# Outer products of two token tiles: one block-diagonal product of 128 rows, or two products of 64 rows

## What is computed

```
scores, idx = top_k(sim, K)                       # 8 of 32 keys, in each of two halves
all_scores = scores[0][..., :, None] + scores[1][..., None, :]
all_idx = idx[0][..., :, None] * NK + idx[1][..., None, :]
sc, pk = top_k(all_scores, K)
indices = take_along_axis(all_idx, pk)            # 64 experts of a token (8 heads x 8)
hmid = einsum('bnd,bnhkd->bnhk', inputs, down[indices])
hmid = sigmoid(sc) * gelu(hmid)
out = einsum('bnhk,bnhkd->bnd', hmid, up[indices])
```

## Time and profile before

| | |
|---|---|
| median of 3 runs | 543.69 us (541.75 to 544.99) |
| profiled execution | 543.2 us, span 541.4 us |
| busy, share of the span | PE 82%, PEld 64%, DVE 75%, ACT 40%, POOL 27% |
| experts, from the first to the last spread | 338.7 to 532.0 us |
| one steady duo | 32.0 us |
| matmuls of the spread | 2 x 896 in the records, mean 192 ns each from start to end |

### The profile page before, as it was taken

One profiled execution on the slowest core, in us unless ns is written; L12 is line 12 of the kernel. 1 busy time (PEld: TensorE's weight loads), 2 busy tenths in 40 slices (PEclk: granted clock), 3 DMA queues, 4 the chain that ended last, 5 costly groups with the idle time before them and its releaser, 6 DMA issues. The chain is left out here.

```text
span 541.4 us, 14245 instructions
## 1 busy us (share of the span) xinstructions
PE 442.6 (82%) x5223; PEld 348.8 (64%) x5223; DVE 407.6 (75%) x1693; ACT 216.7 (40%) x401; POOL 147.4 (27%) x206
## 2 busy tenths in 40 slices
PE   1889999978999999999998534967849587684867
PEld 1667777765688687787777222756638376573767
DVE  2899999967455465455466699999899979999571
ACT  1454554566445345345464304232242423224230
POOL 1343334430000000000000153461726537163600
PEclk9999999999999999999998858585765858668596
DMA  9991000010356646646100000000000000000000
GB/s 222 219 217 48 0 0 0 10 70 1 95 136 146 193 116 163 177 114 179 49 2 1 0 1 0 4 10 3 12 1 3 10 2 10 1 11 2 3 11 11
DMA packets 8730, 30.51 MB, mean 56 GB/s; under 512 B 696, under 2 KB 4280, under 8 KB 8408
## 3 DMA queue, kind: packets, MB, share of 16 engines
q1 hardware_dynamic: 8680, 29.89, 21.9%
HBM read 28.97 MB, written 0.92 MB: 55 GB/s over the span
## 5 line engine op out<-in xcount | busy, mean ns | idle before, releaser
L1274 PE MATMUL PS<-b_hi,AR 128*128 128x16 f16 x896 | 54.8, 192 | 25.0 <-DVEq L936 25.0
L1274 PEld LDWEIGHTS PS<-b_hi,AR 128*128 128x128 f16 x896 | 54.0, 108 | 29.0 <-DVEq L936 29.0
L1244 PE MATMUL PS<-xlT,KB 128*128 (+1 forms) x112 | 35.1, 467 | 26.9 <-ACT AR L594 22.1
L1275 PE MATMUL PS<-b_lo,AR 128*128 128x16 f16 x896 | 54.7, 192 | 0.0
L1275 PEld LDWEIGHTS PS<-b_lo,AR 128*128 128x128 f16 x896 | 54.1, 107 | 0.0
L1244 PEld LDWEIGHTS PS<-xlT,KB 128*128 128x128 f32 x112 | 24.5, 230 | 38.3 <-ACT AR L594 24.9
L1070 PE MATMUL PS<-KA,AR 125*128 125x125 f32 x384 | 46.8, 272 | 0.8 <-ACT AR L417 0.8
L343 POOL TENSOR_TENSOR xn<-xn,cexp 128x1280 f16<-128x1280 f16 x14 | 41.8, 2985 | 17.8 <-DVE xn L907 17.8
L1154 PE MATMUL PS<-AR 125*64 125x128 f32 x768 | 46.6, 279 | 0.0
L1136 PE MATMUL PS<-AR 128*64 128x500 f32 x192 | 43.8, 591 | 1.3 <-ACT XA L499 0.9
L1070 PEld LDWEIGHTS PS<-KA,AR 125*128 125x128 f32 x384 | 41.6, 141 | 4.7 <-issue 3.5
(11 more groups left out here) (146 smaller groups left out, 980.6 us busy)
## 6 DMA issues: line engine op xcount, KB each, us to landing
AR<-ctx SPq DMA_DIRECT2D x16, 1344.0 KB
AR<-ctx SPq DMA_DIRECT2D x16, 156.0 KB
KB<-pack_b SPq DMA_DIRECT2D x1, 1280.0 KB, 13.6
XA<-pack_q SPq DMA_DIRECT2D x1, 1024.0 KB, 4.7
KA<-pack_a SPq DMA_DIRECT2D x1, 965.0 KB, 6.8
XA<-x SPq DMA_DIRECT2D x4, 224.0 KB
out<-res SPq DMA_DIRECT2D x7, 128.0 KB, 1.8
XA<-zeros SPq DMA_DIRECT2D x2, 64.0 KB
```

The lines of the kernel that those rows point to most:

```text
L1244: last = mm(bank(6 + r % 2, k * 256, k * 256 + 256), wb("down")[:, v * U:(v + 1) * U], xlT[:, bass.ds(i * 2 * TILE, 2 * TILE)], **one)
L1274: mm(o, pick_u[:, n, :], b_hi[:, :, n], start=True, stop=False)
L1275: last = mm(o, pick_u[:, n, :], b_lo[:, :, n], start=False, stop=True)
```

## The change

The two tiles' outer products are computed apart. `b_hi` and `b_lo` shrink to 8 columns per n and have no zero quarters, so POOL's two fills go and DVE fills each with one instruction over 128 partitions. For each n `spread` issues four matmuls: b_hi for rows 0 to 63, b_hi for rows 64 to 127, then both for b_lo. Each loads 64 rows of pick_u (128 columns) as weights and has 8 columns. The first tile's results go to banks 0 and 1, the second's to banks 2 and 3, 64 n in each bank. ACT's four copies and DVE's last scaling follow that layout: the copies keep their number and size; the scaling becomes four instructions of 512 elements for eight of 256, behind two signals for four.

```diff
-        b_hi = sb("b_hi", [128, 2 * V, TILE], F16)
-        b_lo = sb("b_lo", [128, 2 * V, TILE], F16)
+        b_hi = sb("b_hi", [128, V, TILE], F16)
+        b_lo = sb("b_lo", [128, V, TILE], F16)
...
-            ch.did(nc.gpsimd.memset(b_hi[:, :, :], 0.0))
-            ch.did(nc.gpsimd.memset(b_lo[:, :, :], 0.0))
...
             def mix_copies(i):
                 act.wait_ge(s["mix_psum"], i + 2)
                 for b in range(4):
-                    last = nc.scalar.activation(act_w[:, :, :, b * 32:(b + 1) * 32].rearrange("p t v n -> p (t v) n"),
-                                                bank(b).rearrange("p (n w) -> p w n", w=2 * V), ACT.Copy, scale=1.0 / W_UP)
+                    last = nc.scalar.activation(act_w[:, b // 2, :, (b % 2) * 64:(b % 2) * 64 + 64],
+                                                bank(b).rearrange("p (n v) -> p v n", v=V), ACT.Copy, scale=1.0 / W_UP)
...
-                for t in range(2):
-                    for dst, w in ((b_hi, w_hi), (b_lo, w_lo)):
-                        r = slice(t * HK, (t + 1) * HK)
-                        ch.did(nc.vector.tensor_tensor(dst[r, t * V:(t + 1) * V, :], pick_v[r, :, :],
-                                                       w[r, :].rearrange("p (o n) -> p o n", o=1).to_broadcast([HK, V, TILE]), ALU.mult))
+                for dst, w in ((b_hi, w_hi), (b_lo, w_lo)):
+                    ch.did(nc.vector.tensor_tensor(dst[:, :, :], pick_v[:, :, :],
+                                                   w[:, :].rearrange("p (o n) -> p o n", o=1).to_broadcast([128, V, TILE]), ALU.mult))
...
-            for b in range(4):
-                dve.wait_ge(s["bank_spread"], b + 1)
+            for half in range(2):
+                dve.wait_ge(s["bank_spread"], half + 1)
                 for t in range(2):
-                    n0 = (DUOS - 1) * 2 * TILE + t * TILE + b * 32
+                    n0 = (DUOS - 1) * 2 * TILE + t * TILE + half * 64
                     last = nc.vector.scalar_tensor_tensor(
-                        act_w[:, t, :, b * 32:(b + 1) * 32], bank(b).rearrange("p (n t v) -> p t v n", t=2, v=V)[:, t], 1.0 / W_UP,
-                        gelu[:, :, n0:n0 + 32], ALU.mult, ALU.mult)
+                        act_w[:, t, :, half * 64:half * 64 + 64], bank(2 * t + half).rearrange("p (n v) -> p v n", v=V), 1.0 / W_UP,
+                        gelu[:, :, n0:n0 + 64], ALU.mult, ALU.mult)
...
                 for n in range(TILE):
-                    o = bank(n // 32, (n % 32) * 16, (n % 32) * 16 + 16)
-                    mm(o, pick_u[:, n, :], b_hi[:, :, n], start=True, stop=False)
-                    last = mm(o, pick_u[:, n, :], b_lo[:, :, n], start=False, stop=True)
-                    if by_bank and n % 32 == 31:
+                    for dst, stop in ((b_hi, False), (b_lo, True)):
+                        for t in range(2):
+                            r = slice(t * HK, (t + 1) * HK)
+                            last = mm(bank(2 * t + n // 64, (n % 64) * V, (n % 64) * V + V), pick_u[r, n, :], dst[r, :, n],
+                                      start=not stop, stop=stop)
+                    if by_bank and n % 64 == 63:
                         last.then_inc(s["bank_spread"], 1)
```

More of the change, by code:

```diff
@@ L951, in _ @@
             with dve.Fori(0, (DUOS - 1) // 2) as i:
-                ch.enter(i, 2 * (2 * (16 + 16 + 4 + 8 + 8) + 3 + 2 + 4 + U // V - 1))
+                ch.enter(i, 2 * (2 * (16 + 16 + 4 + 8 + 8) + 3 + 2 + 2 + U // V - 1))
                 for j in range(2):
@@ L959, in _ @@
             dve.wait_ge(s["h_done"], (V // 2) * DUOS)
-            for b in range(4):
-                dve.wait_ge(s["bank_spread"], b + 1)
+            for half in range(2):
+                dve.wait_ge(s["bank_spread"], half + 1)
                 for t in range(2):
-                    n0 = (DUOS - 1) * 2 * TILE + t * TILE + b * 32
+                    n0 = (DUOS - 1) * 2 * TILE + t * TILE + half * 64
                     last = nc.vector.scalar_tensor_tensor(
-                        act_w[:, t, :, b * 32:(b + 1) * 32], bank(b).rearrange("p (n t v) -> p t v n", t=2, v=V)[:, t], 1.0 / W_UP,
-                        gelu[:, :, n0:n0 + 32], ALU.mult, ALU.mult)
-                    last.then_inc(s["mixed" if b == 3 else "dve"], 1)
-                    ch.n += b < 3
-                if b == 2:
+                        act_w[:, t, :, half * 64:half * 64 + 64], bank(2 * t + half).rearrange("p (n v) -> p v n", v=V), 1.0 / W_UP,
+                        gelu[:, :, n0:n0 + 64], ALU.mult, ALU.mult)
+                    last.then_inc(s["mixed" if half else "dve"], 1)
+                    ch.n += 1 - half
+                if half == 0:
                     ch.wait()
```

## The result

| | before | after |
|---|---|---|
| median of 4 runs | 543.61 us (541.75 to 544.99) | 548.98 us (548.63 to 549.29) |
| profiled span | 541.4 us | 547.4 us |
| busy, share of the span | PE 82%, DVE 75%, POOL 27% | PE 79%, DVE 72%, POOL 27% |

The ratio is 1.0101, with a 95% interval of 1.0070 to 1.0132: slower by 1.0%, 5.4 us where 21 were forecast. In the changed kernel the spread is L1272, the two products that fill b_hi and b_lo are L927, pick_u is L930, POOL's hit is L341 (L343 before) and its `mix` L353 (L355 before).

A forecast was written before the change was run, and what follows sets the result against it. It took DVE's chain, held by POOL's `mix`, to bound the pass. Terms -1.33 + 8.7 + 5.74 + 8.0 = +21.1 us on the 543.2 us profiled run gave 564.3, hence about 564.8 us by the median; range 536 to 576.

The forecast's parts named there:

- Nothing overlaps there. I therefore take 30.0 ns per pair: PE's spread: row halves do not run side by side, so 512 load-and-matmul pairs take 15.38 us against 7.69.
- Rival B: PE's spread at a pace between, 23 to 28 ns per pair: 11.8 to 14.3 us, total 540 to 557; chance 0.08.
- Rival A: PE's row halves overlap, the spread stays 7.7 us, only DVE's gain is left: 534.5 us; chance 0.20.
- The chain by `mix`: Steady pass from spread start s: POOL's `mix` follows the longer spread, ends at s + 22.33, holds DVE; pass 33.82 against 32.08.
- rival C: The spread doubles but the later `mix` does not hold DVE; picks start earlier, total 553 to 558 us; chance 0.09.
- The working: Step-by-step timing of spread, copies, `mix`, keys and picks, giving a steady pass of 33.82 us at a 15.38 us spread.
- first spread: Start of the first duo's spread: earlier by 1.33 us through DVE's two fewer instructions.
- five steady passes: The five like passes from one spread's start to the next: +1.74 us each, +8.7 in all.
- sixth pass: The shorter pass before the last spread: later `mix` delays picks by 7.07 us, less 1.33, so +5.74.
- tail: After the last spread's start: the spread lies bare, +7.69, and the final scaling adds at most 0.34; +8.0 us.
- The slope of 7 us per us of spread: Each microsecond of spread counts seven times: in five passes, the sixth and the end of the run.
- the break-even of 24.2 ns: PE's pace per pair at which the forecast's sign turns, a spread of 12.37 us.

The follow-up runs named there:

- the run with 8 columns: The kernel before with TensorE's loop over duos 1 to 6, one duo per pass, each spread matmul using only 8 of its 16 columns; 541.29 us.
- before in the same loop: The kernel before, with TensorE's loop over all duos 1 to 6, one duo per pass; 541.80 us, ratio to before 0.9979.
- the four products come back: The changed kernel with TensorE's loop over all duos 1 to 6, VectorE again making the factors in four 64-partition products; 542.60 us, ratio to before 1.0009.
- the block kernel: Changed kernel, TensorE looping one duo per pass; except in the last duo, the spread does all first-half-row products, then all of the other half; 555.41 us.
- the run with half of `mix`: The kernel with one duo per pass and the spread's row halves in blocks, with POOL's `mix` multiplying only half of its columns; 540.38 us.
- the kernel with two duos per pass: The changed kernel with TensorE's loop over all duos 1 to 6, written as three passes of two duos instead of one duo per pass; 549.93 us.
- the loop of one duo: The changed kernel with TensorE's loop written with one duo per pass instead of two, duos 1 to 4 in it; 543.09 us, ratio to before 1.0004.

## Why the prediction was wrong, step by step

**The step that failed: "Nothing overlaps there. I therefore take 30.0 ns per pair".** The spread's term was mis-sized in two ways, one against the other: forecast 15.38 us, measured 11.7 to 13.1. First, the array takes 13.3 ns per matmul, not 30.0, and the spread is 6.8 us where the instructions are there. The rows that I took for the nearest were pairs on alternating *column* halves in f32; row halves in f16 do overlap. Whether the type or the kind of tile makes that difference, no run shows. The Trainium skill (TensorEngine Tiling (Array Packing), Key Properties) says that different tiles load and multiply in parallel; for row tiles the traces agree, 13.3 ns in alternation against 26.5 in blocks. I gave that rule 0.20, on rows of another kind of tile.

Of the 30.0 ns itself 3.4 belong to the 8 columns that fell away, as the run with 8 columns shows; I had read that 16 columns cost nothing.

Second, no term stood for fetching instructions. The doubled count doubled what has to be brought in, and TensorE's loop no longer stayed in place. The holes turned 6.8 us into about 12.4. The warning was in the change's own count, 512 pairs for 256, which I used for the array alone.

**Rival B's time came for a reason that B didn't have.** B had pairs at 23 to 28 ns and 540 to 557 us; the last spread's 12.34 us / 512 gives 24.1 ns, and the time was 549. But that is a mean of 13.3 and of standing still.

**Rival A was right as a mechanism.** With resident code the halves overlap, and 535.95 us stands beside A's 534.5. Its reason holds too, DVE's gain: the step from 541.80 (before in the same loop) to 535.95 is lost whole when the four products come back (542.60).

**DVE loses two instructions, 1.33 us per duo: right.** Passes of 30.60 to 30.74 us where instructions are resident, 31.94 to 32.08 with four products.

**The chain by `mix`: right in kind, short in size.** The forecast says that POOL's L343 "comes after `mix` and still falls on L931, as before". It falls there, but its end comes later, at s + 26.45 below and s + 27.20 in the block kernel for s + 24.25 before, and holds b_lo or the first of the last picks. Duo 0 of after, POOL and then DVE, answering to the earlier trace rows:

```profile
350.68 4.66 POOL L353 TENSOR_TENSOR x<-x,AR 128x1024 f32<-128x1024 f32 x2 [4.31 <-ACT x L580]
...
359.46 2.72 POOL L341 TENSOR_TENSOR xn<-xn,cexp 128x1280 f16<-128x1280 f16 x1
```
```profile
353.00 2.38 DVE L913 TENSOR_SCALAR ev<-eT 128x128 uint16<-128x128 uint16 x1
...
359.15 0.79 DVE L927 TENSOR_TENSOR b_lo<-pick_v,w_lo 128x1024 f16<-128x1024 f16 x1
359.86 7.49 DVE L930 TENSOR_SCALAR AR<-eu 128x1024 f16<-128x1024 uint16 x15
```

L913 is held by `mix` until 355.38, as forecast (so rival C falls here). Then L341 holds the first of the fifteen L930, which take 7.49 us in place of 5.12. The working gives 33.82 - (15.38 - 12.30) = 30.74 for this pass; it took 31.73, and duo 4 the like. The block kernel, whose spread comes nearest to the forecast one, shows the same, 32.0 by the working and 33.1 measured, and there the run with half of `mix` shows that this chain is the reason. For after itself that is carried over from the same rows, not tried.

**Three passes of after are longer still, 32.5 to 33.0.** Behind the spread of duo 2 TensorE's loop of two duos jumps back, and PE waits 3.67 us ahead of L1253, the transpose of the weights, so DVE gets the weights late and its picks wait (6.07 us). It is the wait that the kernel with two duos per pass has at its jumps; in the loop of one duo, which stays in place, it is 0.2 us. In duo 1 DVE's jump and the hold by `mix` add up, as shown above. In duo 3 the spread is the longest, 13.07: the working gives 31.51, and the pass takes 0.96 more, as duos 0 and 4 do. Timeline of PE in duo 2, then of DVE at the jump in duo 1 and at the wait for the weights in duo 2:

```profile
416.62 0.47 PE L1253 MATMUL PS<-KA,weight 128*128 128x128 f32 x1 [3.67 <-issue]
```
```profile
379.23 1.66 DVE L877 MAX8 val<-PS 128x8 f32<-128x32 f32 x16 [3.66 <-issue]
...
421.20 0.29 DVE L912 SCALAR_TENSOR_TENSOR w_lo<-PS,w_hi 128x128 f16<-128x128 f32 x1 [6.07 <-ACT w_hi L599]
```

**The sum, term by term** (spans, us):

| term | forecast, spread 15.38 | the same working at the measured spread | measured |
|---|---|---|---|
| first spread | -1.33 | -1.33 | -2.97 |
| five steady passes | +8.7 | 8.7 - (5 x 15.38 - 62.42) = -5.8 | +1.46 |
| sixth pass | +5.74 | 5.74 - (15.38 - 11.74) = +2.1 | +2.18 |
| tail | +8.0 | 8.0 - (15.38 - 12.34) = +5.0 | +5.33 |
| sum | +21.1 | 0.0 | +6.0 |

So 21 us of the forecast hung on the spread's length, and the sixth pass and the tail follow the working to 0.4 us. The five passes miss by 7 us for the reasons above. The slope of 7 us per us of spread and the break-even of 24.2 ns hold only while nothing else waits: at a mean of 24.1 ns the kernel was 5.4 us slower. The first spread came 1.6 us earlier than DVE's two instructions explain; it starts at 333.8 to 335.8 in all kernels with two products and 337.1 to 338.7 in those with four. Why it is that much stays open.

## What to carry to other kernels

Count instructions, not only array time: where the count of small matmuls doubles, ask whether the loop's code still stays in place, and look for waits that "issue" ends and for packets on the instruction queue. If it doesn't stay, a shorter loop body can give back more than the edit itself: 14 us here, by writing one duo per pass in place of two. And price an edit on one engine by undoing the other engine's half: here PE gained 0.8 us per spread that no steady pass needed, and the gain was that of two VectorE instructions.

## What the runs showed of the hardware

- Matmuls on the two row halves (64 rows, 128 weight columns, f16, 8 moving columns, a weight load each) run side by side when they alternate: a pair starts every 26.7 ns, 13.3 ns per matmul; in blocks of one half it is 26.5 ns per matmul.
- 8 columns start 26.6 ns apart and 16 columns 30.0, at a granted clock of 0.50 in both the earlier trace rows. I had read from equal paces at two clocks that columns cost nothing; they cost 3.4 ns here.
- TensorE's code came in packets of 16.3 KB, 128 load-and-matmul pairs each by the length of a burst. Between the ends of bursts lay 3.1 to 4.0 us in the spread shown first, and every hole ended 2.3 to 2.9 us after a packet's start. The Trainium skill (Runtime: NRT & Kernel Launch, Instruction fetch mechanics) gives blocks of 16 KiB and 256 instructions, with which the bursts agree, and calls the cost of a block's boundary mostly hidden: that held at 26.5 ns per matmul (no holes in one run, two of 0.3 us in another) and not at 13.3 (1.2 to 2.4 us each).
- Loops of about 1140 and 1250 instructions on TensorE ran their later passes without waits for code, and one of about 2280 did not. The same section gives TensorE room for 2048 instructions, with which this agrees; it also says that a jump out of the two current blocks stalls, which the first two loops, four blocks long and more, didn't show on TensorE (0.2 us at each jump of the one of 1140), while the one of 2280 waited up to 3.7 us.
- VectorE's loop jump cost 2.6 us with four products per duo and 3.5 to 3.8 with two, in every kernel here. Packets of 8 KB on the other instruction queue (q14) go with it: at the first jump DVE goes on 3.2 us after such a packet has started, in before and in after, but in before the packet starts 0.6 us ahead of the last instruction's end and in after 0.4 us behind it. Why it starts later was not tried.
